# A transformer block on one core: sums of x moved to POOL, the last MLP items' norm split, copies and a maximum moved up

## What is computed

```
k, v  = LN(ctx; lnkv) @ wk + bk,  LN(ctx; lnkv) @ wv + bv
slots = q_mu + exp(q_logsig) * norm(x)
3 times:
    q     = LN(slots; lnq) @ wq + bq
    attn  = softmax(k q^T * sqrt(D)) over the slots, + 1e-8, divided by its sum over the keys
    slots = attn^T v @ wu + bu + slots
    slots = gelu(LN(slots; lnm) @ w1 + b1) @ w2 + b2 + slots
    slots = LN(slots + cond; lnp)              # (s - mean) * rstd * lnp_g + lnp_b
x   = x + slots
out = x + LN(gelu(norm(x) @ tern(W_fc)); ln_w, ln_b) @ tern(W_proj)
```

## Time and profile before

| what | us |
|---|---|
| median of three runs | 335.87 |
| the profiled execution, its own time | 337.69 |
| its span, first to last instruction | 335.6 |
| PE busy | 316.7 |
| DVE busy | 277.8 |
| ACT busy | 228.0 |
| POOL busy | 214.2 |

### The profile page before, as it was taken

The page is one execution under the profiler, slowest core; times in us unless marked ns, Lnnn a source line. Parts: engine busy times, 40 slices in busy tenths (PEclk is TensorE's granted clock), DMA queues, the critical chain, the costliest instruction groups (busy, mean ns, idle before and its releaser), DMA issues. The chain is left out here.

```text
span 335.6 us, 6157 instructions
## 1 busy us (share of the span) xinstructions
PE 316.7 (94%) x1758; PEld 261.8 (78%) x1758; DVE 277.8 (83%) x816; ACT 228.0 (68%) x504; POOL 214.2 (64%) x417
## 2 busy tenths in 40 slices
PE   8999999999999999999998998999894989999995
PEld 8888887888888888888887777887671767777774
DVE  2799967989899999999998999887678388888763
ACT  2368985967667878587599474865566386777871
POOL 3169866265679755666987646678766856566331
PEclk9999999999999999999999999999999699999999
DMA  7989000000000000000000000000000000000001
GB/s 283 314 281 401 11 1 0 0 2 0 1 3 0 1 3 0 2 2 0 2 0 0 3 0 2 3 0 2 0 0 0 3 32 33 32 31 2 32 33 63
DMA packets 5312, 13.24 MB, mean 39 GB/s; under 512 B 672, under 2 KB 672, under 8 KB 4896
## 3 DMA queue, kind: packets, MB, share of 16 engines
q1 hardware_dynamic: 4160, 10.88, 9.0%
q10 hardware_dynamic: 1120, 1.98, 1.6%
HBM read 10.76 MB, written 2.10 MB: 38 GB/s over the span
## 5 line engine op out<-in xcount | busy, mean ns | idle before, releaser
L285 DVE BATCH_NORM_STATS2 stats<-S 128x6 f32<-128x256 f32 x112 | 42.1, 417 | 9.1 <-DMA S<-ctx 3.6
L336 PE MATMUL ps_mid<-XT,KT 128*128 128x256 f32 x192 | 46.0, 383 | 3.4 <-ACT XT L352 3.4
L336 PE MATMUL ps_low<-V,PR 128*128 128x257 f32 x192 | 46.1, 382 | 0.9 <-DVE PR L877 0.6
L336 PE MATMUL ps_mid<-XT,wt 128*128 128x256 f32 x192 | 45.6, 380 | 0.8 <-ACT XT L352 0.7
L336 PE MATMUL ps_low<-wn,GT 128*128 128x256 f32 x192 | 45.4, 379 | 0.0
L336 PEld LDWEIGHTS ps_low<-V,PR 128*128 128x128 f32 x192 | 36.1, 190 | 7.4 <-DVE PR L877 2.5
L336 PEld LDWEIGHTS ps_mid<-XT,KT 128*128 128x128 f32 x192 | 34.6, 190 | 8.5 <-ACT XT L352 4.8
L336 PEld LDWEIGHTS ps_low<-wn,GT 128*128 128x128 f32 x192 | 36.2, 190 | 4.9
L303 POOL TENSOR_TENSOR lnm_ab<-lnm_mv,mhalf 128x2 f32<-128x2 f32 x24 | 17.3, 721 | 35.7 <-DVE lnm_mv L293 35.7
L336 PEld LDWEIGHTS ps_mid<-XT,wt 128*128 128x128 f32 x192 | 34.7, 190 | 5.1 <-ACT XT L352 1.2
L352 ACT ACTIVATE XT<-ps_t 128x512 f32<-128x512 f32 x56 | 33.0, 590 | 8.2 <-PE ps_t L328 8.2
(11 more groups left out here) (127 smaller groups left out, 708.9 us busy)
## 6 DMA issues: line engine op xcount, KB each, us to landing
S<-ctx SPq DMA_DIRECT2D x8, 256.0 KB, 3.9
X<-x SPq DMA_DIRECT2D x8, 256.0 KB, 4.0
out<-X SPq DMA_DIRECT2D x8, 256.0 KB, 2.0
rowv<-rows SPq DMA_DIRECT2D x1, 1920.0 KB, 9.9
wf<-w_fc_t SPq DMA_DIRECT2D x1, 1024.0 KB, 11.9
wf<-w_proj_t SPq DMA_DIRECT2D x1, 1024.0 KB, 13.6
wt<-w_tr ACTq DMA_DIRECT2D x1, 512.0 KB, 4.2
wn<-w_nat ACTq DMA_DIRECT2D x1, 512.0 KB, 5.5
```

Source lines behind the costliest of these rows:

```text
L285: dve.bn_stats(ln.st[:, at, j, 0:6], tiles[:, j]).then_inc(ln.stats_done, 1)
L336: last = pe.matmul(dst(m), lhs_t[:, c, m * P:(m + 1) * P], rhs[:, c, 0:n], start=(c == 0), stop=(c == 1))
```

## The change

1. `X + lnp_b` moves from DVE to POOL, one 128x512 operation an item, with the row `lnp_b` read for both halves: items 0 to 3 in steps 19 to 22 of round 0, items 4 to 7 in steps 7 to 10 of round 1. DVE's `shift_x` is gone.
2. For item 7 of rounds 0 and 1, DVE no longer centres. POOL makes both coefficients (three small operations instead of one), ACT applies them to `S` with scale and bias (L312's form), and POOL multiplies by `lnp_g` in one 128x512 operation ahead of its two sums.
3. ACT applies MLP item 6's norm in step 18, behind the copy of attention item 2, instead of at the end of step 17 ahead of it.
4. In step 19 DVE takes the maximum of attention item 2 ahead of scaling item 1.

```diff
+SHIFT_X = {(0, STEPS + 3 + k): k for k in range(4)} | {(1, LEAD + k): 4 + k for k in range(4)}
...
+        def both_rows(r):
+            return r[:, None, :].broadcast_to([P, J2, D])
...
-        def ln_coef(pool, ln, n, at, shift=True):
+        def ln_coef(pool, ln, n, at, shift=True, turn=None):
...
-            pool.wait_ge(ln.chain, n * 2 + 2)
+            pool.wait_ge(ln.chain, (n if turn is None else turn) * 2 + 2)
...
                 for r, half, b in staged(t, s, LOW, last):
-                    ln_coef(pool, lnp if half else lnm, r * B + b, b, shift=not half)
+                    if half and b == B - 1 and r < ROUNDS - 1:
+                        ln_coef(pool, lnp, r * B + b, b, turn=r)
+                    else:
+                        ln_coef(pool, lnp if half else lnm, r * B + b, b, shift=not half)
...
                     if half == 1:
-                        pool.wait_ge(p_scaled, r * (J2 * B) + (J2 * b + J2))
+                        if b == B - 1 and not last:
+                            pool.wait_ge(p_unit, r + 1)
+                            pool.tensor_tensor(XH[:, b], XH[:, b], both_rows(row("lnp_g")), ALU.mult).then_inc(p_weighted, 1)
+                            pool.wait_ge(p_weighted, r + 1)
+                        else:
+                            pool.wait_ge(p_scaled, r * (J2 * (B - 1)) + (J2 * b + J2))
                         if last:
-                            pool.wait_ge(x_shifted, J2 * b + J2)
+                            pool.wait_ge(x_shifted, b + 1)
...
                 if not last:
                     norm_coefs(t, s, last)
+                if not last and (t, s) in SHIFT_X:
+                    k = SHIFT_X[t, s]
+                    pool.tensor_tensor(X[:, k], X[:, k], both_rows(row("lnp_b")), ALU.add).then_inc(x_shifted, 1)
                 if it := item(t, s, 5, last):
...
             def apply_norms(t, s, last):
-                if not last and s in (STEPS + 2, STEPS + 3):
-                    s = {STEPS + 2: -1, STEPS + 3: STEPS + 2}[s]
+                if not last and s in (STEPS + 1, STEPS + 2, STEPS + 3):
+                    s = {STEPS + 1: -1, STEPS + 2: STEPS + 1, STEPS + 3: STEPS + 2}[s]
...
+                    elif b == B - 1 and not last:
+                        ln_apply(act, lnp, r * B + b, b, S[:, b], XH[:, b], p_unit)
...
                     copy_xt(act, ring(r, half, b), b % 2)
+                if s == STEPS + 2 and not last:
+                    apply_norms(t, s, last)
...
-                if read_first:
+                if read_first and (last or s != STEPS + 2):
                     apply_norms(t, s, last)
...
-                if s in (LEAD, LEAD + 1):
-                    shift_x(s - LEAD + 5)
-                if s == LEAD + 4:
-                    shift_x(B - 1)
...
                     bn_sum(dve, lnp, r * B + b, b)
-                    centre_gain(dve, lnp, r * B + b, b, S[:, b], XH[:, b], row("lnp_g"), p_gained)
 
                 mid, high = item(t, s, 1, last), item(t, s, 2, last)
+                third = not last and s == STEPS + 3
+                if third:
+                    row_max(mid)
...
-                if mid and mid[1] == 0 and not (change or behind):
+                if mid and mid[1] == 0 and not (change or behind or third):
                     row_max(mid)
...
-                if t == ROUNDS - 2 and s >= STEPS + 2 and not last:
-                    shift_x(s - STEPS - 2)
```

More of the change, by code:

```diff
@@ L173, in build @@
         p_scaled = sem("p_scaled")
+        p_unit = sem("p_unit")
+        p_weighted = sem("p_weighted")
         y_ready = sem("y_ready")
@@ L618, in apply_norms @@
                         ln_apply(act, lnm, r * B + b, b, S[:, b], XH[:, b], xm_ready)
+                    elif b == B - 1 and not last:
+                        ln_apply(act, lnp, r * B + b, b, S[:, b], XH[:, b], p_unit)
                     else:
                         act.wait_ge(lnp.coef, r * B + (b + 1))
-                        act.wait_ge(p_gained, r * (J2 * B) + (J2 * b + J2))
+                        act.wait_ge(p_gained, r * (J2 * (B - 1)) + (J2 * b + J2))
                         for j in range(J2):
@@ L829, in ffn @@
                     low_parts(b + 1, 1 - u)
-            def shift_x(b):
-                for j in range(J2):
-                    dve.tensor_tensor(X[:, b, j], X[:, b, j], row("lnp_b"), ALU.add).then_inc(x_shifted, 1)
             def before_tail(s):
```

## The result

The changed kernel takes 337.05 us (median of 20 runs, 336.48 to 339.05), the kernel before 335.76 in the 20 runs made beside them (334.78 to 338.14): 1.3 us slower. The ratio is 1.0046, with a 95% interval of 1.0027 to 1.0065. The forecast was 336.9.

A forecast was written before the change was run, and what follows sets the result against it. PE was taken to bound the kernel, busy for 316.7 of 335.6 us, its waits in the round changes being for ScalarE's copies. Terms of +1.5, +2.1 and -2.6 made +1.0 on the 335.87 median: 336.9, range 334.2 to 338.6.

The forecast's parts named there:

- First change: First round change: item 7's longer chain (+0.8), POOL's sums of x (+1.4) and PE's restarts (0.1) cost +1.5 us.
- the 0.8 isn't kept: Round changes, item 2's product: the moved copy gains 0.8, but item 4's copy follows a norm waiting for DVE's moments.
- the signs: Expected evidence: item 2's wait near 0.2, items 5 and 6 waiting 0.6 and more, comparisons in steps 7 to 11 at 0.9 to 1.3.
- Steps between the changes: From step 7 of round 1: POOL's sums hold DVE's comparisons up by 2.8; after slack, PE waits +2.1 us more.
- POOL has room for 4 x 1.27 here too: Steps 7 to 10 of round 1: POOL can take four sums of x at 1.27 each; DVE may lack room.
- the +1.2 that the rule would have added: Steps 7 to 11 of round 1: full-instruction blocking would cost six meetings of sums and comparisons 0.2 more each, +1.2.
- Second change: Second round change: DVE loses the x sums, 3.47 us; item 7's chain (+0.8) and restarts (0.1) leave -2.6.
- the 3.47: Second round change's extra length over the first, with the same 222 matmuls: called waiting and credited to DVE's x sums.
- A: Rival, chance 0.2: POOL's sums don't hold DVE up between the changes; 2.1 becomes 0, the sum -1.1, 334.8 us.
- B: Rival, chance 0.08: ScalarE and POOL hide item 7's chain and the x sums, copies keep their gain; -5.1, 330.8 us.
- C: Rival, chance 0.17: blocks of comparisons last to the sum's end, or sums take 1.46; total +2.3, 338.2 us.
- D: Rival, chance 0.05: the parts cancel over the whole kernel, 335.9 us.

The follow-up runs named there:

- e1: The changed kernel with the sums of x back on DVE; item 7's new norm, the moved copies and the third maximum stay. 336.22 us, ratio 1.0014.
- e5: The kernel before with only the moved copies and the third maximum; sums of x and item 7's norm as before. 336.19 us, ratio 1.0011.
- e9: e4 plus pairs of unread 128x2 powers on POOL in steps 7 to 10 of round 1, where the sums had stood. 335.69 us, ratio 1.0009.
- e4: The changed kernel with items 4 to 7's sums of x in steps 7 to 10 of the last round instead of round 1. 335.16 us, ratio 0.9976.
- e2: The changed kernel with only the sums of x on POOL; item 7's norm, copies and third maximum as before. 335.50 us, ratio 1.0004.
- e6: The kernel before with only the sums of x on POOL, in steps 21 and 22 and the last round's 7 to 10. 332.73 us, ratio 0.9912.
- e8: e7 with item 7's norm split over ScalarE and POOL, as in the change. 332.02 us, ratio 0.9891.
- e10: The changed kernel with each sum of x on POOL behind that step's S sum instead of ahead of it. 335.72 us, ratio 0.9994.
- e7: e6 with the moved copies, and in step 18 DVE makes query item 5's moments ahead of MLP item 7's. 331.20 us, ratio 0.9864.

## Why the prediction was right, and where its reasons were not

The three terms came out at +1.42 (+1.5 predicted), +2.18 (+2.1) and -2.28 (-2.6), the sum at +1.32 (+1.0). The sizes were met; of the reasons, two were not as written, and it is in part luck that the sum is so near.

**First change.** The chain ran as it was written down. Item 2's wait fell to 0.19, and at item 4's product PE was still 0.52 ahead. POOL's multiply started at 124.25 (124.3 predicted), took 1.27 (1.3), the two sums followed at 125.59 (125.9), item 6's coefficients at 127.02 (127.3), item 5's copy at 130.10 (130.4) and PE at 130.73 (131.0). Counted from the start of the stretch, which lies 0.10 earlier in the changed kernel, item 5's product came 0.59 late, where +0.8 was written. Item 6's copy ended at 135.09 instead of 135.6, which cost 1.1 instead of 1.4; 0.3 of gaps behind it, where 0.1 had been set down, made up for that. e1 puts the split and the moves together at 0.69 and e5 the moves alone at 0.10, as the step "the 0.8 isn't kept" said. Of what was priced too low, DVE's scaling at 125.31 took 1.16 instead of the 0.62 that it takes at 130.91: it ran beside POOL's multiply and sums. Of the signs, two came out otherwise: item 6's wait is 0.25, not 0.6 and more, and of the ten comparisons of steps 7 to 11 five take 0.92 to 1.41 and five 0.33 to 0.59.

**Steps between the changes.** The size was right, and so were the hold-ups: the comparisons at 139.65 and 144.49 lost 0.98 where 0.95 was predicted, and the eight pairs took 3.0 longer, against 2.8. What failed is the step "POOL has room for 4 x 1.27 here too". POOL had idle time enough in sum, but in the steps where it mattered it stood in pieces shorter than a sum. The timeline of POOL in the kernel before:

```profile
149.37 0.70 POOL L303 TENSOR_TENSOR lnm_ab<-lnm_mv,mhalf 128x2 f32<-128x2 f32 x1 [0.62 <-DVE lnm_mv L293]
...
152.42 0.70 POOL L303 TENSOR_TENSOR lnm_ab<-lnm_mv,mhalf 128x2 f32<-128x2 f32 x1 [0.53 <-DVE lnm_mv L293]
...
154.30 0.69 POOL L301 TENSOR_TENSOR lnp_ab<-lnp_mv,mhalf 128x2 f32<-128x2 f32 x1 [0.73 <-DVE lnp_mv L293]
```

e9 shows it: without a hold-up beside the four sums' places, 1.23 of the 1.91 is still there. The comparisons' waiting was counted as if all of it went into DVE's chain; a part of it lay in time in which POOL was late by itself. And the first 0.5 of it, at 139.65, comes from item 3's sum, one of the first change's four: e4 keeps that hold-up and has no wait. Two causes, one overestimated and one left out, met the right sum: that +2.1 came so near +2.18 is luck.

**The end of a hold-up.** POOL's sum at 139.55 ends by the record at 140.82. The comparison at 139.65, with its own 0.33 at the end, went on at 139.65 + 1.31 - 0.33 = 140.63, 0.2 sooner, as the prediction had read from the earlier trace rows. The Trainium skill, SBUF — State Buffer, section Who interferes with whom, states that the engine that issues first keeps the port pair for the whole instruction. These rows agree but for the last 0.2; the measurement decides, and the +1.2 that the rule would have added does not show. Whether POOL let go before its work ended, or its recorded end is late, stays open.

**Second change.** The prediction says of the 3.47 "that is waiting" and "I let the 3.47 go with them", the sums. By the earlier trace rows PE's idle time is 3.05 there against 1.18 in the first change, 1.87 more; the other 1.60 stands in the rows as a busy PE, whose products at 197.39, 201.65, 205.91 and 213.28 of the kernel before begin 0.25 to 0.29 late with no wait named. And not all of the waiting is the sums'. The timeline of PE in the kernel before, items 2 and 4 of the second change:

```profile
182.17 1.99 PE L336 MATMUL ps_mid<-XT,KT 128*128 128x256 f32 x8 [1.11 <-ACT XT L352]
...
190.94 1.99 PE L336 MATMUL ps_mid<-XT,KT 128*128 128x256 f32 x8 [0.70 <-ACT XT L352]
```

Without the sums, in e2, waits of 1.13 and 0.49 are still there, and 3.03 came back (3.16 in e6). The split with the moves took 0.75 (0.8 predicted); by itself, in e8, it takes 0.34. This is the term that was mis-sized, by 0.3.

**Rivals.** A falls by the comparisons of 1.31 and by the wait; e9 adds that it would have been wrong in its price too, since with no hold-up beside those places PE still waits 1.23. B falls by item 5's copy. C falls by the 1.27 of the sums and by the 0.2 above. D falls by the interval of the ratio, though the parts do cancel to a good part: -2.28 against +3.60.

## What to carry to other kernels

Work that is moved to an engine with idle time needs a place where that idle time lies in one piece and is not on someone's chain: the same eight sums gave a ratio of 1.0004 where half of them stood among POOL's short gaps and DVE's comparisons (e2) and 0.9912 where they filled POOL without making PE wait and no comparison lost time to one (e6). How much of that is the gaps' and how much the comparisons', these two runs don't say. Something read a round later or more belongs behind what is read in the next step; swapping two statements was worth 1.05 us of the stretches here (e10). And when a shorter step only makes the next one wait, as the moved copies did, move the producer of that next one as well: with item 5's moments ahead the same copies kept their 0.6 to 0.7 in each change (e7).

## What the hardware showed that was not expected

An operation on POOL of 128x512 in which one row of 256 is read for both halves takes 1.27 (L490, L511), no more than L447 in the earlier trace rows without that reading, and 0.2 less than two of 128x256 (1.46). Two powers of 128x2 on POOL take 1.34 together and don't hold a DVE comparison up that starts 0.11 behind the first (e9's 144.50, 0.33), while an undivided sum of 1.27 holds it for 0.98. The hold goes the other way too: in e10 a sum of x at 150.14, begun 0.05 behind a comparison (150.09, 0.47), took 1.54 instead of 1.27. A lead of 0.10 decides which of the two stands still: the sum has it at 139.65 of the changed kernel, the comparison at 138.66 of e6.

Behind the same 4.0 us wait of PE in the tail the granted clock was 0.63 over the next 7.80 us in the profiled execution of the kernel before and 0.74 over the next 6.57 in that of the changed one, means of time at 0.50 (1.2 GHz) and at 1.00 (2.4 GHz): PE had run at 1.00 up to the wait in both. What decides how long the lower level lasts was not tried.
